# Both gates of the state-space mixer as one Silu activation, and a new order of the calls

## The reference, cut to what matters

```python
xz = jnp.einsum('btd,ed->bte', x, in_proj_w)
x_in, z = (xz[..., :Dd], xz[..., Dd:])
...                                   # causal convolution of x_in, 4 taps: x_c
x_conv = jax.nn.silu(jnp.swapaxes(x_c, 1, 2))          # first gate
ssm_params = jnp.einsum('btd,ed->bte', x_conv, x_proj_w)
B_ssm = ssm_params[..., :N]; C_ssm = ssm_params[..., N:2 * N]
dt = jax.nn.softplus(ssm_params[..., -1:] * dt_proj_w[None, None, :, 0] + dt_proj_b)
dA = jnp.exp(dt[..., None] * A[None, None])
dBx = dt[..., None] * B_ssm[:, :, None, :] * x_conv[..., None]
...                                   # h = dA*h + dBx over time, 16 states; y = sum over states of h*C
y = y * jax.nn.silu(z)                                 # second gate
```

## Time and profile before

| | us |
|---|---|
| median of 3 runs | 961.75 (959.28 to 962.03) |
| time of the profiled execution | 961.2 |
| its span | 959.4 |
| VectorE busy | 802.2 (84%) |
| TensorE busy | 796.9 (83%) |
| ScalarE busy | 671.6 (70%) |
| GpSimd busy | 561.4 (59%) |

### The profile page before, as it was taken

How to read it: one execution, slowest core, us unless ns; L and a number is a source line. 1 busy time by engine, 2 the same in 40 slices (tenths; PEclk the granted TensorE clock), 3 DMA queues, 4 the chain that set the end, 5 groups by cost and what they waited for, 6 DMA issues and landing times. The chain is left out here.

```text
span 959.4 us, 9608 instructions
## 1 busy us (share of the span) xinstructions
PE 796.9 (83%) x2802; PEld 528.2 (55%) x2802; DVE 802.2 (84%) x1013; ACT 671.6 (70%) x1345; POOL 561.4 (59%) x468
## 2 busy tenths in 40 slices
PE   2385867978987799999899999998998797787585
PEld 1264644736554556475647564756476546546464
DVE  5245566677799999999999999999999999989761
ACT  4347687588767865997699769876976685465452
POOL 0202457437836793789378937893776376565421
PEclk9597977989998889999999999999999799789597
DMA  9000000000100010001000100010000000000000
GB/s 315 12 23 22 23 1 22 1 1 0 56 1 0 1 42 13 0 1 59 8 1 1 60 1 0 1 46 0 1 1 27 1 1 1 23 0 1 22 1 22
DMA packets 10341, 19.49 MB, mean 20 GB/s; under 512 B 1457, under 2 KB 5297, under 8 KB 10289
## 3 DMA queue, kind: packets, MB, share of 16 engines
q1 hardware_dynamic: 10288, 18.88, 5.8%
HBM read 14.69 MB, written 4.19 MB: 20 GB/s over the span
## 5 line engine op out<-in xcount | busy, mean ns | idle before, releaser
L385 POOL TENSOR_TENSOR y<-y,hC 128x1024 f32<-128x1024 f32 (+3 forms) x140 | 280.1, 2001 | 77.3 <-DVE hC L1461 73.4
L1914 PE MATMUL pC<-w,hT 128*128 128x256 f32 x1024 | 232.4, 382 | 4.9 <-ACT hT L754 4.9
L819 ACT ACTIVATE dA<-dt,A_neg 128x512 f32<-128x512 f32 (+3 forms) x320 | 187.5, 630 | 54.3 <-DVE hs L1450 53.8
L1914 PEld LDWEIGHTS pC<-w,hT 128*128 128x128 f32 x1024 | 194.5, 191 | 36.7 <-issue 7.2
L1450 DVE TENSOR_TENSOR_SCAN hs<-dA,carry,pS 128x512 f32<-128x512 f32 (+3 forms) x192 | 193.4, 1008 | 18.1 <-ACT dA L819 10.4
L2037 PE MATMUL pS<-stack,sel 97*128 97x512 f32 (+3 forms) x320 | 148.0, 515 | 54.5 <-DVE hs L1450 54.0
L1435 DVE TENSOR_TENSOR pS<-u,pS 128x1024 f32<-128x1024 f32 (+3 forms) x160 | 159.8, 999 | 17.4 <-PE pS L2037 16.8
L1461 DVE TENSOR_TENSOR hC<-hs,pS 128x1024 f32<-128x1024 f32 (+3 forms) x160 | 157.5, 985 | 15.3 <-PE pS L2037 15.1
L1450 DVE TENSOR_TENSOR_SCAN hs<-dA,pS 128x512 f32<-128x512 f32 (+1 forms) x128 | 138.2, 1080 | 14.6 <-POOL carry L392 6.0
L754 ACT ACTIVATE hT<-pA,ffb_sb 128x512 f32<-128x512 f32 (+3 forms) x160 | 94.7, 599 | 59.2 <-PE pA L1907 58.9
L1907 PE MATMUL pA<-tg,w 128*128 128x512 f32 (+3 forms) x320 | 127.9, 538 | 7.7 <-ACT hT L754 6.3
(11 more groups left out here) (120 smaller groups left out, 1101.5 us busy)
## 6 DMA issues: line engine op xcount, KB each, us to landing
xt<-xT SPq DMA_DIRECT2D x6, 515.0 KB, 4.7
xtok<-x SPq DMA_DIRECT2D x6, 512.0 KB, 5.3
out<-x3b SPq DMA_DIRECT2D x6, 512.0 KB, 2.9
w<-w1a SPq DMA_DIRECT2D x1, 1024.0 KB, 8.3
w<-w2a SPq DMA_DIRECT2D x1, 1024.0 KB, 10.4
w<-w1b SPq DMA_DIRECT2D x1, 1024.0 KB, 8.3
w<-w2b SPq DMA_DIRECT2D x1, 1024.0 KB, 9.9
xt<-xT SPq DMA_DIRECT2D x2, 259.0 KB, 7.8
```

What stands on the lines that cost most here:

```text
L385: nc.gpsimd.tensor_tensor(y[:, :, 0:ch.T], so_far, hC[:, n % CRING, :, 0:ch.T], ALU.add).then_inc(S["y_sum"], 1)
L819: nc.scalar.activation(dA[:, k % ARING, 0:ch.T], dt[ch.side][:, h, 0:ch.T], ACT.Exp, scale=A_neg[:, h, n:n + 1]).then_inc(S["dA_ready"], 1)
L1914: mm = nc.tensor.matmul(dst[:, b * D:b * D + D], src(k, t0), w[:, k, :], start=k == 0, stop=k == nk - 1)
```

## The change

`z_tanh` and `mconv_tanh` become `z_silu` and `mconv_silu` on ScalarE, with the function Silu; VectorE's two products go away, and with them two semaphores. The factors 0.5 go away too. As nothing on VectorE reads the old `zz` any more before ScalarE overwrites it, `z_silu` waits for the read-out of the chunk two before. The order of the calls within each of the four variants is another one on ScalarE, VectorE, TensorE and GpSimd; the instructions are the same otherwise.

```diff
-            def z_tanh(ch, h):
+            def z_silu(ch, h):
+                if ch.i > 1:
+                    act.wait_ge(S["yg_ready"], ch.i - 1)
                 act.wait_ge(S["z_mm"], H * ch.i + h + 1)
-                nc.scalar.activation(zz[ch.side][:, h, 0:ch.T], pC[h][:, 0:ch.T], ACT.Tanh, scale=0.5).then_inc(S["tz_ready"], 1)
+                nc.scalar.activation(zz[ch.side][:, h, 0:ch.T], pC[h][:, 0:ch.T], ACT.Silu).then_inc(S["zz_ready"], 1)
...
-                nc.scalar.activation(v[:, :, 0:ch.T], cv[:, :, 0:ch.T], ACT.Tanh, scale=0.5).then_inc(S["tcv_ready"], 1)
+                nc.scalar.activation(v[:, :, 0:ch.T], cv[:, :, 0:ch.T], ACT.Silu).then_inc(S["v_ready"], 1)
...
-                nc.scalar.mul(stack[ch.side][0:NXK, 0:ch.T], pA[0][0:NXK, 0:ch.T], 0.5).then_inc(S["stack_hi"], 1)
+                nc.scalar.copy(stack[ch.side][0:NXK, 0:ch.T], pA[0][0:NXK, 0:ch.T]).then_inc(S["stack_hi"], 1)
...
-            def z_silu(ch, h):
-                dve.wait_ge(S["tz_ready"], 2 * ch.i + h + 1)
-                V.scalar_tensor_tensor(out=zz[ch.side][:, h, 0:ch.T], in0=zz[ch.side][:, h, 0:ch.T], scalar=1.0, in1=pC[h][:, 0:ch.T],
-                                       op0=ALU.add, op1=ALU.mult).then_inc(S["zz_ready"], 1)
-
-            def mconv_silu(ch):
-                dve.wait_ge(S["tcv_ready"], ch.i + 1)
-                V.scalar_tensor_tensor(out=v[:, :, 0:ch.T], in0=v[:, :, 0:ch.T], scalar=1.0, in1=cv[:, :, 0:ch.T], op0=ALU.add,
-                                       op1=ALU.mult).then_inc(S["v_ready"], 1)
...
-                V.scalar_tensor_tensor(out=u[:, :, 0:ch.T], in0=dt[ch.side][:, :, 0:ch.T], scalar=0.5, in1=v[:, :, 0:ch.T], op0=ALU.mult,
-                                       op1=ALU.mult).then_inc(S["u_ready"], 1)
+                V.tensor_tensor(u[:, :, 0:ch.T], dt[ch.side][:, :, 0:ch.T], v[:, :, 0:ch.T], ALU.mult).then_inc(S["u_ready"], 1)
...
-                V.scalar_tensor_tensor(out=yg[:, :, 0:ch.T], in0=y[:, :, 0:ch.T], scalar=0.5, in1=zz[ch.side][:, :, 0:ch.T],
-                                       op0=ALU.mult, op1=ALU.mult).then_inc(S["yg_ready"], 1)
+                V.tensor_tensor(yg[:, :, 0:ch.T], y[:, :, 0:ch.T], zz[ch.side][:, :, 0:ch.T], ALU.mult).then_inc(S["yg_ready"], 1)
```

More of the change, by code:

```diff
@@ L893, in entry @@
                         state_decay(scan, 1)
+                if gate is not None:
+                    gate_tanh(gate, 0, 0)
+                if scan is not None:
+                    if scan.i > 0:
+                        state_decay(scan, 2)
                 if tail is not None:
@@ new lines, in entry @@
+                if gate is not None:
+                    gate_tanh(gate, 1, 1)
+                    decays(gate)
+                if prep is not None:
+                    to_channel_major(S["x2T_mm"], pA[1], x1T, S["x2T_ready"], prep, 1)
+                if tail is not None:
+                    normalize(LN_Y, tail, x3)
+                if gate is not None:
+                    root_ln(gate)
+                if tail is not None:
+                    x3_channel_major(tail, 0, gate)
+                if gate is not None:
+                    root_exp(gate)
@@ new lines, in entry @@
+                if scan is not None:
+                    if scan.i > 0:
+                        state_decay(scan, 5)
+                if tail is not None:
+                    x3_channel_major(tail, 1, gate)
+                if prep is not None:
+                    mconv_input(prep, 0)
+                    mconv_input(prep, 1)
+                    mconv_first(prep, tail)
+                if tail is not None:
+                    relu(1, tail, 0, prep)
+                if prep is not None:
+                    mconv_tap(prep, 1)
@@ new lines, in entry @@
+                if tail is not None:
+                    relu(1, tail, 7)
+                if prep is not None:
+                    x_proj_high(prep)
+                if ahead is not None:
+                    conv_first(ahead)
+                if prep is not None:
+                    step_sizes(prep)
+                if scan is not None:
+                    state_decay(scan, 9)
+                    state_decay(scan, 10)
+                if ahead is not None:
+                    conv_tap(ahead, 1, prep)
@@ new lines, in entry @@
+                if ahead is not None:
+                    conv_tap(ahead, 2, prep)
+                if gate is not None:
+                    relu(0, gate, 2)
+                if scan is not None:
+                    state_decay(scan, 14)
+                if gate is not None:
+                    relu(0, gate, 3)
+                    relu(0, gate, 4)
+                if scan is not None:
+                    state_decay(scan, 15)
+                if gate is not None:
+                    relu(0, gate, 5)
@@ L1148, in step @@
                     relu(0, gate, 7)
+                if ahead is not None:
+                    conv_tap(ahead, 3, prep)
                 if tail is not None:
@@ L1571, in entry @@
                         state_output(scan, 1)
+                if gate is not None:
+                    clip_log_decay(gate)
+                if scan is not None:
+                    if scan.i > 0:
                         state_scan(scan, 2, 1)
@@ L1660, in entry, with closing @@
                     state_scan(scan, 15, 1)
-            def step(ahead, gate, prep, scan, tail):
+            def closing(ahead, gate, prep, scan, tail):
+                if prep is not None:
+                    history(prep)
+                    add_ffn0(prep, 0, tail)
                 if scan is not None:
@@ L1805, in closing @@
                     state_scan(scan, 1, 1)
-                if tail is not None:
-                    readout(tail, gate)
-                if scan is not None:
                     state_input(scan, 2)
@@ L2124, in entry @@
                         spread_B(scan, 1)
+                if gate is not None:
+                    gate_mm(gate, 0, 0)
+                    gate_mm(gate, 0, 1)
+                if scan is not None:
+                    if scan.i > 0:
                         spread_C(scan, 0)
```

1008 lines of the change are left out of this document (459 added, 549 removed).

## The result

| | us |
|---|---|
| median of 4 runs, before | 960.5 (958.95 to 962.03) |
| median of 4 runs, changed | 1004.3 (1003.62 to 1007.05) |
| ratio | 1.046, 95% interval 1.043 to 1.049 |
| forecast | 956, range 946 to 968 |

A forecast was written before the change was run, and what follows sets the result against it. VectorE was taken as the bound in steps 4 to 9, TensorE close behind. 961.2 - 13.5 + 2.2 + 3.0 + 2.3 = 955.2 us, 955.8 with 0.55 for the median, stated as 956; range 946 to 968.

The forecast's parts named there:

- VectorE's loss of work: Steps bound by VectorE: the products of `z_silu` and `mconv_silu` gone, 2.34 us per chunk of 512, 13.5 us in all.
- the edges: Opening and steps 2, 3 and 10: added loads partly hidden, +2.3 us in sum, between -1 and +8; step 10 alone -0.9.
- What bounds the kernel: Steps 4 to 9: VectorE is the bound, TensorE close behind; 1 us less on VectorE is up to 1 us of time.
- Rival 2: TensorE takes over in steps 4 to 9, VectorE's 11 us net come down to 2 to 3; 961 us, chance 0.20.
- Scans behind their `state_input`: Steps 4 to 9: 9 states in place of 7 have the scan right behind its product, 0.18 us each, +2.2 us.
- The loads' count: ScalarE, whole kernel: 78 table loads in place of 43, each 1.283 us with no drain, 44.9 us more busy time.
- waits of at most 0.5 us a step: Steps 4 to 9: late factors from ScalarE's loads make VectorE wait 0.5 us a step, 3.0 us for six.
- 10.6 us more: Four more loads a step at the skill's 2.66 us each, called beyond what ScalarE has left; rejected for the measured gap.
- Rival 1: ScalarE becomes the bound at s6, s7 and s10 of `step`, 2.6 us a step; 973 us, slower, chance 0.22.

The follow-up runs named there:

- run 2: Old order of calls, Tanh as the gates' function without VectorE's products (wrong gate values, 43 loads), against the kernel before: 953.8 us, ratio 0.993.
- run 6: Changed kernel with three waits on GpSimd in `step`, and Tanh in place of Silu (wrong gate values, 35 loads gone): 971.9 us, ratio 1.010.
- run 4: Changed kernel with three waits in `step`: GpSimd waits for `a2_minus_1`, `gate_input` and the recurrence before its sums: 979.6 us, ratio 1.020.
- run 3: Changed kernel with Tanh in place of Silu (wrong gate values, 43 loads in place of 78), order and waits unchanged: 1001.75 us, ratio 1.043.
- run 5: Kernel before with one wait: in `step` GpSimd's sum of state 5 waits for `scaled_input`, so that it starts beside the recurrence: 981.5 us, ratio 1.020.
- run 9: Kernel before with one of eight hidden blocks left out of the second product of both feed-forward layers on TensorE: 952.7 us.
- run 10: Old order, Tanh without VectorE's products, one of eight hidden blocks left out of TensorE's second feed-forward products: 943.7 us.
- run 7: Changed kernel with the three GpSimd waits, but `entry` (steps 2 and 3) in the old order on all four engines: 974.4 us, ratio 1.013.
- run 12: Silu and the three GpSimd waits, new order in `step` alone; `opening`, `entry` and `closing` in the old order: 979.6 us, ratio 1.018.
- run 1: Old order of calls on every engine, with Silu in place of Tanh and product (82 loads), against the kernel before: 991.0 us, ratio 1.032.
- run 11: Changed kernel with the three GpSimd waits and one of eight hidden blocks left out of TensorE's second feed-forward products: 973.1 us.

## Why the prediction was wrong

The step that failed is one that the sum has no term for: VectorE's loss of work (-13.5) was taken with all its other calls at their old durations, and the new order was priced by what stands next to what on one engine at a time. The collisions with GpSimd that this put at nothing measured +25 us. The terms beside it were mis-sized too: the products -6.5 in place of -13.5, and the order of the edges, +2.3 in the forecast, some +16. The account, by medians:

| step | us | from |
|---|---|---|
| kernel before | 960.5 | |
| products gone from VectorE | -6.5 | run 2 |
| the order, above all in steps 2 and 3 | +18 | run 6 less run 2 |
| table loads in that order | +8 | run 4 less run 6 |
| three collisions with GpSimd in `step` | +25 | changed less run 4 |
| changed kernel | 1004.3 | |

The sizes hold for this order of taking the parts away. With no loads in the kernel the same three waits are worth 30 us (run 3 less run 6), and with the collisions in it the loads are worth 2.5 (run 3).

Point by point:

- **What bounds the kernel: half right.** VectorE is the bound of the steps from 4 on: 26 us more or 21 us more on it arrive nearly whole (runs 4 and 5). But in the other direction 1 us less was not 1 us of time.
- **The products, -13.5: mis-sized.** They measure 6.5 (run 2), most of it in step 4, of which 2.0 is a collision that went away. In the middle step nothing was won: waits of VectorE for ScalarE's `root_exp` and `stack`, which no rival named, took the place of the products. Rival 2's TensorE hides a part at most, 2.5 us by the medians, no more than their uncertainty (runs 9 and 10).
- **Scans behind their `state_input`, +2.2:** about right. In steps 4 to 9, 60 scans start right behind their product in place of 49, each some 0.25 us later than it could: +2.7. The listed waits of this kind over the whole span are 11.2 us and 7.0 before, so +4.2.
- **The loads' count, 78, and each one's length, 1.283 us with no drain: right.** That they bring waits of at most 0.5 us a step in `step`: right in the changed kernel (no wait for line 821 in the middle step). Over steps 4 to 9, where 3.0 us were forecast, it is 1.3 us longer than run 3, and run 4 is 3.7 us longer than run 6. In the old order the loads would have cost 37. One comparison in the forecast was wrong, though nothing came of it: 10.6 us more would not have been beyond what ScalarE had left in the middle step, which was 15 us (93 less 77.8).
- **The edges, +2.3 (-1 to +8): wrong.** Steps 2 and 3 alone have +16, and step 10 has +3.7 (70.2 in place of 66.5) where -0.9 was forecast. I had summed only loads there. The trace of step 2 shows TensorE's transposes ahead of rows not yet normalized, and steps 2 and 3 have collisions of 3.3 us on VectorE; how much each of them costs is not shown. Of the 16, 4.5 us are `entry`'s own order (run 7) and 3.9 more that of `opening` (run 12); the other 7.5 come with Silu in the old order of these steps (173.2 us in run 1). In the new order the loads are worth only 1.1 us there (run 6, 180.2 in place of 181.3): so the losses by the loads and by the order are not a sum; each hides part of the other.
- **Rival 1 (slower, 973)** had the right sign and the wrong mechanism: VectorE has no wait for line 821 in the changed kernel's middle step, and all 35 loads are worth 2.5 us there (run 3).
- **Missing altogether: the collisions, +25 in steps 4 to 9.** Their trace was there before the change: in the kernel before, GpSimd's sum takes 3.28 us in place of 2.37 beside `gate_input`, and the recurrence of step 4 takes 4.5 us. To have seen them, one had to lay VectorE's and GpSimd's new orders beside each other in time.

Two things stay open. One is the mechanism of the order's 18 us, of which 16 lie in steps 2 and 3. The other is which of the small waits sets the middle step at 95.8 to 96.9 us in the kernel before and in runs 2, 4, 6, 7, 11 and 12: no single wait of VectorE exceeds 1.4 us in it (2.3 in run 11), and cutting TensorE's work shortened it by 1.4 at most.

## What to carry to other kernels

When calls are reordered, list for each VectorE call with all its inputs in SBUF what GpSimd does at that moment. A collision cost up to the whole of each GpSimd call that it met: here 1.2 us for `gate_input`, 2.1 for a recurrence that met one call whole and 4.2 for one that met two, on an engine that is the bound. A wait put on GpSimd can pay for itself. A busy time that grows while the count of instructions falls was the sign of it. Before crediting an instruction removed from the busiest engine, look at who arrives last for the next one: in this kernel, with VectorE and TensorE over 80% busy, half of the saving was worth nothing.

## What the runs showed of the hardware

- VectorE and GpSimd shut each other out in turns: two scans of 1.23 us beside two GpSimd calls of 2.37 us took 6.64 us, and the second GpSimd call 3.25. A scan over time with its inputs in SBUF is one of the calls that did this. So is a one-input call: `a2_minus_1`, 0.66 us for 1024 columns alone, took 1.95 us beside a sum. The same section of the Trainium skill counts `tensor_scalar` in its two-port mode among the calls that exclude GpSimd, and that agrees.
- The calls with one operand in PSUM (`state_output` and `state_input`, 1.2 us) kept their time beside GpSimd's sums in every trace.
- Silu takes a table load in and one out when it stands between activations of Exp: 19 loads stand at the Silus, and 35 more in all.
